# Sorting the tokens of a top-2 expert layer in two halves, and weaving the first half's expert tiles into the routing of the last groups

## What is computed

```python
x = x + tanh(g_xattn[0]) * attention_16_heads(layernorm(x), ctx_768)
x = x + tanh(g_ffn[0])   * mixture_of_6_experts_of_width_64(layernorm(x))   # all experts run on all tokens
x = x + tanh(g_xattn[1]) * attention_1_head(layernorm(x), ctx_768)
x = x + tanh(g_ffn[1])   * _L1_ffn_ref(layernorm(x), Wg, W1, W2, W3)

def _L1_ffn_ref(x, Wg, W1, W2, W3):          # E = 8, TOP_K = 2, D = 128, H = 256
    logits = x @ Wg
    top_vals, top_idx = top_k(logits, 2)
    weights = scatter of softmax(top_vals) to the two experts
    for e in range(E):
        u, v = x @ W1[e], x @ W2[e]
        out = out + ((u * sigmoid(u) * v) @ W3[e]) * weights[..., e][..., None]
```

## Time and profile before

| | us |
|---|---|
| median of 3 runs | 895.5 (893.76 to 896.17) |
| the profiled execution | 895.98 |
| its span in the trace | 894.1 |
| PE busy | 767.9 (86%) |
| DVE busy | 674.1 (75%) |
| ACT busy | 552.8 (62%) |
| POOL busy | 466.2 (52%) |

### The profile page before, as it was taken

The page is one execution under the profiler, slowest core; times in us unless marked ns, Lnnn a source line. Parts: engine busy times, 40 slices in busy tenths (PEclk is TensorE's granted clock), DMA queues, the critical chain, the costliest instruction groups (busy, mean ns, idle before and its releaser), DMA issues. The chain is left out here.

```text
span 894.1 us, 24977 instructions
## 1 busy us (share of the span) xinstructions
PE 767.9 (86%) x7840; PEld 575.0 (64%) x7840; DVE 674.1 (75%) x2688; ACT 552.8 (62%) x1139; POOL 466.2 (52%) x504
## 2 busy tenths in 40 slices
PE   4999999999999959999998899964199999999900
PEld 2566666666666536677676677654199999999800
DVE  3889889998898958989999988864256555556545
ACT  2777777777777645788888877642155555555400
POOL 3554345544456011247676666776456666666610
PEclk9999999999999969989999988985599999999955
DMA  8101000010000010001111111111333333333279
GB/s 238 44 23 35 30 21 21 21 41 21 21 21 2 3 60 1 10 31 46 43 50 43 40 49 46 51 44 37 111 81 94 95 92 95 94 91 91 66 246 331
DMA packets 56036, 57.57 MB, mean 64 GB/s; under 512 B 9040, under 2 KB 48003, under 8 KB 55971
## 3 DMA queue, kind: packets, MB, share of 16 engines
q1 hardware_dynamic: 37827, 33.71, 13.3%
q0 software_dynamic: 8640, 17.84, 5.9%
q10 hardware_dynamic: 9504, 5.23, 2.0%
HBM read 32.74 MB, written 24.02 MB: 63 GB/s over the span
## 5 line engine op out<-in xcount | busy, mean ns | idle before, releaser
L1562 POOL DMA_INDIRECT contributions<-d_y,d_token x142 | 135.9, 957 | 79.2 <-issue 52.3
L999 POOL DMA_INDIRECT sorted_rows<-r_send,r_slots x128 | 126.8, 990 | 52.9 <-issue 37.9
L1607 DVE TENSOR_TENSOR d_hidden<-d_silu,d_v 128x512 f32<-128x512 f32 x71 | 48.8, 688 | 83.8 <-ACT d_silu L1635 83.8
L428 POOL TENSOR_SCALAR a_k_heads<-a_kT,first 128x512 f32<-128x512 f32 x60 | 93.3, 1573 | 0.8 <-ACT a_kT L479 0.8
L1635 ACT ACTIVATE d_silu<-d_u 128x512 f32<-128x512 f32 x71 | 42.4, 597 | 76.2 <-PE d_v L1655 76.2
L503 ACT ACTIVATE a_probs<-a_scores 128x1024 f32<-128x1024 f32 x64 | 65.6, 1025 | 29.2 <-PE a_scores L603 29.1
L346 DVE TENSOR_REDUCE a_neg_max<-a_scores 128x16 f32<-128x1024 f32 x64 | 78.0, 1219 | 7.1 <-PE a_scores L593 5.6
L510 ACT COPY a_probsT<-a_probsT_bank 128x512 f32<-128x512 f32 x128 | 74.8, 584 | 11.6 <-PE a_probsT_bank L620 11.1
L620 PE MATMUL a_probsT_bank<-first,a_probs 128*128 128x128 f32 x512 | 79.7, 278 | 2.2 <-ACT a_probsT L510 0.3
L343 DVE TENSOR_REDUCE a_denom<-a_probs 128x16 f32<-128x1024 f32 x64 | 77.3, 1208 | 1.7 <-issue 1.3
L1674 PE MATMUL d_y_bank<-d_w,d_hidden 128*128 128x128 f32 x568 | 75.1, 275 | 0.5 <-DVE d_hidden L1607 0.5
(11 more groups left out here) (209 smaller groups left out, 1824.3 us busy)
## 6 DMA issues: line engine op xcount, KB each, us to landing
d_rows<-sorted_rows SPq DMA_DIRECT2D x71, 130.0 KB, 2.2
d_pair<-contributions SPq DMA_DIRECT2D x16, 512.0 KB, 7.0
X<-in_x SPq DMA_DIRECT2D x16, 256.0 KB, 2.9
out_x<-X ACTq DMA_DIRECT2D x16, 256.0 KB, 7.7
ctxT<-in_ctx_T SPq DMA_DIRECT2D x16, 192.0 KB, 2.9
c_ctxT<-in_ctx_T SPq DMA_DIRECT2D x16, 192.0 KB, 2.4
contributions<-d_y,d_token POOLq DMA_INDIRECT x142, 2.3
w<-in_L_ffn_W SPq DMA_DIRECT2D x2, 1024.0 KB
```

Of the source, the lines that this page charges most:

```text
L428: last = pool.tensor_scalar(keys_of_head(par, j), kT[:], c.head_of_group[:, j:j + 1], None, ALU.mult)
L999: pool.indirect_dma_start(dispatch.rows, bass.IndirectOffsetOnAxis(ap=slots[n % 2][:, k, j:j + 1], axis=0), send[n % 2][k][:, j, :], None) ...
L1562: pool.indirect_dma_start(dispatch.contributions, bass.IndirectOffsetOnAxis(ap=token[u][:, h:h + 1], axis=0), shares[u][:, h, :], None).th ...
```

## The change

The tokens are sorted in two halves, groups 0 to 7 and 8 to 15. Each half has its own regions in the DRAM table, its own `next_row`, and its own plan. Tiles are of 128 rows instead of 256, so that each half has 71 tiles (`HALF_TILES`) and the kernel 142. Phase 3 is gone as a block: its work, `sparse(t)`, stands inside phase 2, which is written out only to i = 18; behind that the routing of groups 14 and 15 is written out piece by piece with `sparse(0)` to `sparse(15)` between the pieces. The rest of the tiles follow, all unrolled (before, most of them were in a hardware loop).

```diff
+HALVES = 2
+GH = G // HALVES
+HALF_TILES = 2 * GH * GW // P + E1 - 1
+DTILES = HALVES * HALF_TILES
...
-    STEPS = range(-1, G + 6)
+    STEPS = range(-1, G + 3)
+    KEEP = 32
+    ROWS = 6
+    shares = [c.v_heads[i // (KEEP // 2)][:].rearrange("p g u s -> p (g u s)")[:, i % (KEEP // 2) * D:i % (KEEP // 2) * D + D]
+              for i in range(KEEP)]
+    PAIRS_AT, ADDS_AT = 104, 108
...
 SP
+            dispatch.fill_up(sp, 0)
+            for t in range(0, DTILES, 4):
+                if t == 0:
+                    sp.wait_ge(dispatch.planned, 1)
+                    sp.wait_ge(dispatch.filled, 16 * (HALVES + E1))
+                if t == 48:
+                    dispatch.fill_up(sp, 1)
+                _, firsts = nc.values_load_multi_w_load_instructions(dispatch.tile_row[0:1, t:t + 4], ...)
+                for n in range(t, min(t + 4, DTILES)):
+                    if n >= ROWS:
+                        sp.wait_ge(row_read, n - ROWS + 1)
+                    sp.dma_start(rows[n % ROWS][:], dispatch.rows[bass.ds(firsts[n - t], P), :]).then_inc(d_loaded[n % ROWS], 16)
+                if t == PAIRS_AT:
+                    blocks_kept(sp, HALF_TILES // 4 + 1)
+                if PAIRS_AT <= t < PAIRS_AT + 4 * GH:
+                    load_pair((t - PAIRS_AT) // 4)
+            blocks_kept(sp, -(-DTILES // 4))
+            for g in range(GH, G):
+                load_pair(g)
...
 POOL, behind all its iterations of phase 2
+            for b in range(-(-DTILES // 4)):
+                pool.wait_ge(row_read, tiles[-1] + 1)
+                pool.tensor_copy(token[:, here], ends[:, here, 0]).then_inc(token_ready, 1)
+                wait_alone(pool, token_ready, b + 1)
+                for t in tiles:
+                    wait_alone(pool, share_ready, t + 1)
+                    pool.indirect_dma_start(dispatch.contributions, bass.IndirectOffsetOnAxis(ap=token[:, t % KEEP:t % KEEP + 1], axis=0),
+                                            shares[t % KEEP], None).then_inc(kept[b % 8], 16)
...
 DVE
+            def sparse(t):
+                dve.wait_ge(ends_mm, t + 1)
+                    dve.tensor_copy(xT[t % 4][:], tr_bank(t)[:, 0:P]).then_inc(d_xT_ready, 1)
+                    dve.tensor_scalar(shares[w % KEEP], y_bank[w % 2][:, 0:D], ends[:, w % KEEP, 1:2], None, ...)
+                    dve.wait_ge(silu_done, m + 1)
+                    dve.tensor_tensor(d_hidden[m % 4].rearrange("p k n -> p (k n)"), silu[m % 2], uv[m % 2][:, KH * P:2 * KH * P], ...)
+                    dve.tensor_copy(ends[:, t % KEEP, :], rows[t % ROWS][:, D:ROW]).then_inc(row_read, 1)
+                    dve.tensor_copy(w3[t % 8], c.w3[:, bass.ds(experts[t % 4], 1)].rearrange("p a b d -> p (a b d)")).then_inc(w3_ready, 1)
+                g, q = (t - ADDS_AT) // 4, (t - ADDS_AT) % 4
+                if 0 <= g < GH:
+                    add_piece(g, q // 2, q % 2)
...
             for i in STEPS:
+                if i == G + 2:
+                    dispatch.count_tiles(dve, c, 0)
+                    dispatch.find_experts(dve, c, 0)
+                    dispatch.place_tiles(dve, c, 0)
                 attended(i - 5)
...
 PE
+            def sparse(t):
+                m, w = t - HIDDEN, t - OUT            # HIDDEN, OUT = 2, 4
+                    for i in range(2 * KH):
+                        last = pe.matmul(uv[m % 2][:, bass.ts(i, P)], w12[m % 3][:, bass.ts(i, P)], xT[m % 4][:], start=True, stop=True)
+                        pe.wait_ge(d_xT_ready, t if t <= 16 else t - 1)
+                    last = pe.transpose(tr_bank(t)[:, 0:P], rows[t % ROWS][:, 0:D], c.ident[:])
+                    for k in range(KH):
+                        last = pe.matmul(y_bank[w % 2][:, 0:D], d_hidden[w % 4][:, k, :], w3[w % 8][:, bass.ts(k, D)], ...)
```

571 lines of the change are left out of this document (319 added, 252 removed).

## The result

The changed kernel takes 884.42 us (median; 883.87 to 890.11), the kernel before 895.84 in the runs beside it: a ratio of 0.9887, 95% interval 0.9841 to 0.9933. That is faster, inside the range of 851 to 886, but a third of the gain that was forecast: 11 us in place of 32. The experiments come from five sessions; in three of them (experiments 5 to 12, 17 and 18) the kernel before itself took 957 to 960 us in place of 892 to 897, so each experiment is read against the kernel before of its own session, and in such a session the changed kernel wasn't faster at all (1.0069, experiment 9).

A forecast was written before the change was run, and what follows sets the result against it. PE was taken to bound phase 3's tiles, with a routing hole and a closing pass around them. POOL's end at 839 us + 23.2 closing pass = 862 us span, + 1.9 around it = 864 us; range 851 to 886.

The forecast's parts named there:

- The place of the first tile: Start of the weave: PE's first tile instruction at 604 us, 22 us after the first plan's start.
- the step itself: PE's work on one 128-row tile: 13 instructions of 128 columns at 0.112 us, 1.46 us.
- that POOL and not PE ends last: End of the tiles: POOL's last scatter at 839 us, 8 us behind PE's last weighed result at 831.
- the closing pass behind the last scatter: End of the kernel: eight groups instead of 16 behind the last scatter, 23.2 us instead of 40.25.
- the eight groups under the tiles: Second half's tiles: the first half's closing pass, 4 MB loads and 2 MB stores, hidden by six row buffers.
- The ratio that spoke against small tiles: PE step: the skill's ratio of 1.45 for 128-column matmuls would make a 128-row step 2.0 us; not adopted.
- I take 1.35: POOL's cost per tile, scatter plus a share of the cast and its wait: 1.35 us, between 1.29 and 1.41.
- Loading four expert numbers ... I take 0.5 for four, 0.12 a tile: DVE step: loading expert numbers for each fourth tile costs 0.5 us, 0.12 a tile.
- DVE fits: DVE's work per tile sums to 1.2 us, up to 1.4, within a step of 1.46.
- 6 us, an estimate: Weave of 16 steps with the last routing: PE's waits for DVE's routing blocks, 6 us.
- Number 1: Rival: a longer step of PE or DVE, 1.60 us, decides; kernel at 874 us; chance 0.25.
- Number 2: Rival: POOL's scatters slow beside DVE's new copy, 0.15 us a tile, 21 us; kernel at 885 us; chance 0.12.

The follow-up runs named there:

- 5: Changed kernel with the token numbers cast by VectorE instead of GpSimd, checks kept: 977.32 us, 1.0183 of the kernel before.
- 12: Changed kernel without bounds checks, cast on VectorE, filling transfers in two lots, tiles 0 to 3 scattered early: 954.51 us, 0.9949 of the kernel before.
- 17: Changed kernel with only the token cast moved to VectorE, bounds checks kept, run again: 972.84 us, 1.0178 of the kernel before.
- 18: Changed kernel without bounds checks, with the cast on VectorE and 14 unread matmuls: 955.97 us, 0.9938 of the kernel before.
- experiment 9: Changed kernel run again unedited, in a session where the kernel before took 958.8 us: 962.54 us, 1.0069 of the kernel before.
- Experiment 2: Changed kernel with GpSimd casting row numbers one block of four tiles ahead: 887.51 us, 0.9914 of the kernel before.
- Experiment 14: Changed kernel without bounds checks on the plan's numbers and with the token cast on VectorE: 860.96 us, 0.9631 of the kernel before.
- Experiment 13: Changed kernel with the plan's numbers loaded without bounds checks on SyncE, VectorE and ScalarE: 882.61 us, 0.9866 of the kernel before.
- experiment 16: Changed kernel with 14 added matmuls whose result nobody reads, in TensorE's idle stretches: 883.41 us, 0.9880 of the kernel before.
- experiment 4: Changed kernel without the weave, all tiles behind the last routing on TensorE, VectorE and ScalarE: 893.58 us, 0.9998 of the kernel before.
- 1: Changed kernel run again, nothing edited, kernel before at 892.2 us: 886.56 us, 0.9926 of the kernel before.
- 7: Changed kernel always copying expert 0's weights, no expert number loaded by VectorE or ScalarE: 950.64 us, 0.9939 of the kernel before.
- 10: Changed kernel with the plan's numbers loaded without bounds checks, kernel before at 958.8 us: 947.35 us, 0.9916 of the kernel before.
- 11: Changed kernel without bounds checks and with the cast on VectorE, kernel before at 958.8 us: 953.57 us, 0.9939 of the kernel before.

## Why the prediction was off

**Right.** The place of the first tile (22, measured 23.0), with 5 us for the first plan; the step itself (1.46 for 13 instructions of 128 columns, measured 1.45 wherever nothing is late); that POOL and not PE ends last; the closing pass behind the last scatter (23.2, measured 22.2), and that the eight groups under the tiles are hidden but for 2 us. The ratio that spoke against small tiles (2.0 us a step) isn't seen: the undisturbed step is 1.45 us in every session, and where the mean comes near 2.0 (sessions 2, 3 and 5) it is made of such steps and pauses. Forecast 17 us for the closing pass less its cost, measured 13. That POOL ends 8 us behind PE (measured 9.3) was luck in its size: both ends came 26 us later than forecast, each for a reason of its own.

**The step that failed: "I take 1.35"**, a tile on POOL. It is 1.455 over the first 100 tiles and 1.475 over all 142, as the last ones have scatters beside VectorE's additions and two longer waits (1.1 and 1.6 us): 142 x (1.475 - 1.35) = 17.7 us. The working had both parts, the cast and a late start behind a wait, but priced the wait by one that the engine's own result doesn't end (0.63 us); behind a cast of its own POOL stands idle for 0.82. The bound of 1.41 was too low by the same term. Experiment 2 shows the price on its own: with the wait moved behind other scatters, four tiles cost 5.13 in place of 5.82 us. Experiment 14, which takes the cast from POOL, puts POOL's end at 254.8 us after the plan, where 257 was forecast; that is no confirmation, as its first tile is 4.6 us later than forecast and its tiles cost 1.31 on average.

**The step that hid behind it: "Loading four expert numbers ... I take 0.5 for four, 0.12 a tile"**, and with it "DVE fits". The loads leave DVE idle for 0.81 us and ACT for 0.98, once in four steps, and the two tiles of depth between the engines don't absorb that. It is not DVE alone: the working put ACT aside with "it has room", and PE waits for ACT's late weight copy more (8.6 us) than for DVE's late product (3.7). Experiment 13 shows that it is the checks of the bounds: without them 20.6 us of TensorE's time go away, 2.1 of them in the step at tile 48, where SyncE's queue was late. The working scaled up an idle time of 0.31 us, in which one load (0.32) stands together with one check; the load is paid once for four numbers, the check four times. In the kernel before (ns):

```profile
L1624 ACTq TENSOR_LOAD <-plan_tile_expert x71: 273/321/478, 641.0 to 841.0; - x71
```

The Trainium skill (Runtime: NRT & Kernel Launch, Instruction fetch mechanics) gives about 200 ns for each register in such a load, and speaks of loads from HBM. The plan lies in SBUF here, and a load of four takes 0.34 us with the checks and without; so the measurement decides, and in this kernel the load wasn't the cost.

**The weave: "6 us, an estimate"** of waits. The 17th tile comes 9 us later than forecast, 1 of them already there at the first tile. The half clock behind TensorE's two idle stretches, which the working left out, is worth 6.1 us at that place (experiment 16), 2.2 of them ahead of the first tile and 3.9 in the weave. Of the 8 us that the weave itself took too long some 4 are left, which no experiment took apart. POOL's first tile is as late, 9 us, since the weave holds the last routing group's rows back by 10 us (62.8 in place of 52.5 in experiment 4).

Together 9 + 17.7 = 26.7 us on POOL's end, where 26.4 are missing (283.2 - 256.8). The kernel then misses by 25.6 in the trace and by 20.4 in the medians, as that execution was 5.7 above its own median. The two failed prices don't add up: TensorE's end at 273.9 and POOL's at 283.2 are two bounds of nearly one height, so taking TensorE's away alone gave 3 us in the trace (13; 0.0060 x 896 = 5 by the ratios), and taking both gave 28 in the trace and 26 by the ratios (14 against 1: 0.0295 x 896). Taking POOL's away alone wasn't run in such a session; experiment 2, which takes most of it, gave 3 in the trace, with TensorE's end where it was. That the forecast came out at the time of the kernel with both mended, 861 us, is in part chance, as said above of POOL's end.

**The rivals.** Number 1 (steps of PE or DVE decide) named the register load and had the size of the step: 1.61 on average for its 1.60. It was the second bound: POOL still ended last. Number 2 has a small part: the scatters are longer beside DVE's work, but beside its additions, not beside the new copy. In experiment 14 their mean is 963 ns between 660 and 710 us, with the copy and without additions, and 1123 between 780 and 830 us, with both:

```profile
L1119 POOL DMA_INDIRECT contributions<-v_heads,d_token x41 | 39.5, 963 | 12.5 <-issue 9.4 <-DVE v_heads L1280 3.0
```

```profile
L1119 POOL DMA_INDIRECT contributions<-v_heads,d_token x36 | 40.4, 1123 | 11.0 <-issue 11.0
```

The Trainium skill (GPSIMD Engine Reference, Key points) names both a 2-port mode and two SBUF inputs as what contends; the second agrees with these rows, the first isn't seen. The pair loads also run in the later stretch, but single scatters of the changed kernel's trace tell the two apart. Between 800 and 850 us the 25 that stand beside an addition for 0.15 us or more last 1.046 us on average, the 6 that stand beside none 0.963, some of these with pair loads in flight. Between 680 and 798 us the 22 with no W3 copy beside them last 0.965, and 38 with one beside them 0.967. So it is the additions.

## What to carry to other kernels

Cutting tiles in half doubles what is paid once a tile: a load of a number with its bounds check, a cast with a wait for its own end. Price those from a row in which the engine waits for its own result, ask which part is paid once and which for each number, and look at the burst and not at the mean. And when two engines end within a few us of each other, an edit that frees only one of them shows little; try the pair before giving either up. Where TensorE waits a few us ahead of a dense stretch, some matmuls that nobody reads can be worth it for the clock: 6 us in the trace of experiment 16.

## What the runs showed of the hardware

- A load of four plan numbers with bounds checks leaves VectorE idle for 0.81 us and ScalarE for 0.98. The load alone takes 0.34 us on VectorE's queue, for four numbers together, and is hidden without the checks; each check adds about 0.28 us (experiment 13).
- A GpSimd indirect DMA behind a cast on GpSimd starts 0.82 us after it, behind another indirect DMA 0.30 us.
- A GpSimd scatter of 128 rows lasts 0.96 us, also beside VectorE's copies from SBUF to SBUF; beside VectorE's additions with two inputs in SBUF it lasts 1.05 (changed kernel) to 1.12 (experiment 14) on average.
- In sessions 2, 3 and 5 TensorE's step averages 1.86 to 2.05 us. Most steps are still 1.45 us; pauses of 1.4 to 2.7 us stand between them, in which VectorE and ScalarE are idle too. Unedited kernel, session 3:

```profile
813.77 0.29 DVE L1275 COPY d_xT<-bc_bank 128x128 f32<-128x128 f32 x1 [2.29 <-PE bc_bank L1751]
...
821.41 0.29 DVE L1275 COPY d_xT<-bc_bank 128x128 f32<-128x128 f32 x1 [2.29 <-PE bc_bank L1751]
```

PE's own row ahead of the first of these ends 0.6 us before it (812.58 + 0.61), so what ends the idle time isn't PE's work. The granted clock is 1.00 there, from 775 to 850 us. The chip of session 4 was also that of session 3, so it isn't the chip. The pauses have a rhythm: in experiments 7, 9 and 10 one of 1.9 us each 7.6 us, each fourth step, and in 11 and 12 one of 1.4 us each 5.7 us, each third step; both ways about a quarter of the time. The loads of four numbers come each fourth step in all of these, so the pauses aren't bound to them. No experiment found the cause; it stays open. Since the pauses lengthen the stretch that is dense on TensorE, and the step with the additional VectorE instruction and the checks more than others (5, 17), a kernel tuned in one kind of session can be slower in the other.
